# Attention stage: mask multiplies put ahead of the previous head's normalisation and of the scaling of V on VectorE

## The reference

```python
xn = layernorm(x)                                  # x: (4, 2048, 4096)
q = (xn @ Wq).reshape(B, S, 32, 128)
k, v = split(xn @ Wkv)                             # one key/value head of 128, shared by all 32 heads
scores = einsum('bqhd,bkd->bhqk', q, k) * 128**-0.5
scores = where(causal, scores + slope[h] * (kpos - qpos), -inf)
attn = einsum('bhqk,bkd->bqhd', softmax(scores), v)
W = (w_q - 128) * scales                           # one scale per 32 inputs, (4096, 4096)
out = x + attn.reshape(B, S, 4096) @ Wo + xn @ W.T
```

## Time and profile before

| what | value |
|---|---|
| time, median of two runs | 2699.53 us (2677.26 and 2721.8) |
| profiled execution, its own time | 2493.82 us |
| span of its slowest core (core 4) | 2492.3 us |
| spans of the eight cores | 2461.7 to 2492.3 us |
| granted TensorE clock, mean per core | 0.890 to 0.897 |
| busy, share of the span: TensorE matmuls, VectorE, ScalarE, GpSimd | 79%, 31%, 22%, 4% |
| first and last copy of row sums (line 684), stage C of core 4 | 777.5 and 1432.3 us |

### The profile page before, as it was taken

The page is one execution under the profiler, slowest core; times in us unless marked ns, Lnnn a source line. Parts: engine busy times, 40 slices in busy tenths (PEclk is TensorE's granted clock), DMA queues, the critical chain, the costliest instruction groups (busy, mean ns, idle before and its releaser), DMA issues.

```text
span 2492.3 us, 39192 instructions; the slowest of 8 cores (2461.7 to 2492.3 us)
## 1 busy us (share of the span) xinstructions
PE 1962.0 (79%) x15350; PEld 1429.2 (57%) x15451; DVE 776.1 (31%) x1896; ACT 538.9 (22%) x595; POOL 87.3 (4%) x103
## 2 busy tenths in 40 slices
PE   1555379999996666666666699899995699999999
PEld 1444234444443333333334388788884588888888
DVE  2666200000003555565444411111110544444432
ACT  0111000000003444445555500000000222222221
POOL 0000000000000000010000000000000000000000
PEclk9866689999997677758988899999997899999999
DMA  7432465676550000014000048867774866665522
GB/s 185 153 136 102 58 69 69 73 84 81 68 68 1 1 1 1 1 19 50 1 1 1 1 49 87 84 88 95 101 95 81 176 149 144 141 140 139 142 86 76
DMA packets 218274, 193.04 MB, mean 77 GB/s; under 512 B 9840, under 2 KB 210544, under 8 KB 211824
## 3 DMA queue, kind: packets, MB, share of 16 engines
q0 software_dynamic: 140736, 103.88, 32.8%
q1 hardware_dynamic: 77360, 86.66, 11.5%
HBM read 269.21 MB, written 25.17 MB: 118 GB/s over the span
## 4 chain that ended last, share of the span: by engine, by line
PE 67%; DVE 12%; DMA 8%; ACT 6%; issue 6%; DVEq 0%; ACTq 0%; POOL 0%; SPq 0%; POOLq 0%
PE psD L411 18%; PE psE L882 17%; PE psD L750 16%; PE psC_av L654 6%; ACT expb L551 5%; PE psC_sc L524 4%; DVE vf L506 3%; DMA wpan<-wo 3%; DVE lnst L261 2%; PE psE_tr L840 2%; PE psA_tr L299 2%; DMA wkvb<-wkv 2%; DMA wpan<-wq 2%; DVE xn_tm L280 1%; DMA scalesb<-scales 1%
## 5 line engine op out<-in xcount | busy, mean ns | idle before, releaser
L882 PE MATMUL psE<-wtp,xnt 128*128 128x256 bf16 x4096 | 469.7, 274 | 28.1 <-ACT wtp L850 22.6
L411 PE MATMUL psD<-xnt,wpan 128*128 128x512 bf16 x2007 | 441.7, 380 | 42.8 <-DMA wpan<-wq 40.6
L750 PE MATMUL psD<-wpan,qat 128*128 128x256 bf16 x4096 | 453.4, 275 | 15.2 <-DMA wpan<-wo 14.5
L750 PEld LDWEIGHTS psD<-wpan,qat 128*128 128x128 bf16 x4096 | 403.4, 99 | 65.1 <-issue 15.9
L882 PEld LDWEIGHTS psE<-wtp,xnt 128*128 128x128 bf16 x4096 | 396.6, 98 | 75.7 <-issue 30.6
L551 ACT ACTIVATE expb<-psC_sc 128x1024 bf16<-128x1024 f32 x333 | 327.1, 1013 | 331.9 <-PE psC_sc L524 304.7
L411 PEld LDWEIGHTS psD<-xnt,wpan 128*128 128x128 bf16 x2048 | 200.8, 98 | 283.8 <-issue 43.3
L654 PE MATMUL psC_av<-vf,expb 128*128 128x129 bf16 x1912 | 189.5, 251 | 190.0 <-DVE expb L562 90.3
L850 ACT COPY wtp<-psE_tr 128x1024 bf16<-128x1024 bf16 x128 | 129.0, 1012 | 900.2 <-PE psE_tr L840 900.2
L654 PEld LDWEIGHTS psC_av<-vf,expb 128*128 128x128 bf16 x1912 | 145.8, 113 | 284.0 <-issue 279.4
L524 PE MATMUL psC_sc<-qat,kt 128*128 128x512 bf16 x603 | 226.6, 474 | 6.0 <-issue 3.5
(11 more groups left out here) (49 smaller groups left out, 832.0 us busy)
## 6 DMA issues: line engine op xcount, KB each, us to landing
xblk<-x SPq DMA_DIRECT2D x16, 2048.0 KB, 7.8
wpan<-wq POOLq DMA_DIRECT2D x16, 2048.0 KB, 21.1
wpan<-wo POOLq DMA_DIRECT2D x16, 2048.0 KB, 24.2
wqr<-wqi POOLq DMA_DIRECT2D x32, 1024.0 KB, 10.3
xin<-x SPq DMA_DIRECT2D x128, 128.0 KB, 3.5
out<-outst SPq DMA_DIRECT2D x128, 128.0 KB, 2.1
scr_awo<-awo SPq DMA_DIRECT2D x128, 64.0 KB, 5.0
awin<-scr_awo SPq DMA_DIRECT2D x128, 64.0 KB, 2.8
```

The lines of the kernel that those rows point to most:

```text
L411: ins = e.matmul(psB[:, quarter * 512:(quarter + 1) * 512], wpan[:, bufp * 8192 + dt * 256 + sub * 128: bufp * 8192 + dt * 256 + (sub + 1) ...
L750: ins = e.matmul(psB[:, slot * 512: slot * 512 + 256], qat[:, h * 1024 + qb * 128: h * 1024 + (qb + 1) * 128], wpan[:, bufp * 8192 + h * 2 ...
L882: ins = e.matmul(psE[:, slot * 512: slot * 512 + 256], xnt[:, dt * 1024 + qb * 128: dt * 1024 + (qb + 1) * 128], wtp[:, bufp * 8192 + dt * ...
```

## The change

In each head the three VectorE steps behind evA are recorded in another order. Before: vf, evB, fm(0). After: fm(0), evB, vf. The waits of every step and all other engines' rows stay as they are. evB also stays in the same place relative to ctp.

```diff
--- before.py
+++ after.py
@@ -497,6 +497,7 @@
                 idx0 = r * NH + h
                 bufv = idx0 % 2
                 ve_vf = 0
+                vfb_todo = None
                 if h >= WIDE_H0:
                     def vfb(e, h=h, r=r, kbs=kbs, bufv=bufv):
                         ins = None
@@ -511,7 +512,7 @@
                     vfw = [("ldm", 32), ("ge", ge_ones)]
                     if idx0 >= 2:
                         vfw.append(("pe", last_av[idx0 - 2]))
-                    ve_vf = E.op("vector", vfb, wait=vfw, inc="ve")
+                    vfb_todo = (vfb, vfw)
                 for gi in range(G + 1):
                     if gi < G:
                         grp = groups[gi]
@@ -530,14 +531,6 @@
                         if it == 0:
                             waits += [("se", B_se)]
                         sc_pe = E.op("tensor", smm, wait=waits, inc="pe")
-                        if gi == 0 and pending is not None:
-                            i_p = pending["idx"]
-                            zr_p = E.reserve("ve")
-                            fn_p = pending["evB"]
-                            ve_evB[i_p] = E.op("vector",
-                                               lambda e, fn_p=fn_p, zr_p=zr_p: fn_p(e, zr=zr_p),
-                                               wait=[("ve", se_evA[i_p]),
-                                                     ("pe", pe_ctp.get(i_p - 2, 0))], inc="ve")
                         if gi == min(3, G - 1) and pending is not None:
                             i_p = pending["idx"]
                             pe_ctp[i_p] = E.op("tensor", pending["ctp"],
@@ -632,6 +625,18 @@
                                 fst["g"] = False
                             else:
                                 ge_f[it] = None
+                        if gi == 0:
+                            if pending is not None:
+                                i_p = pending["idx"]
+                                zr_p = E.reserve("ve")
+                                fn_p = pending["evB"]
+                                ve_evB[i_p] = E.op("vector",
+                                                   lambda e, fn_p=fn_p, zr_p=zr_p: fn_p(e, zr=zr_p),
+                                                   wait=[("ve", se_evA[i_p]),
+                                                         ("pe", pe_ctp.get(i_p - 2, 0))], inc="ve")
+                            if vfb_todo is not None:
+                                ve_vf = E.op("vector", vfb_todo[0], wait=vfb_todo[1], inc="ve")
+                                vfb_todo = None
 
                     if gi >= 1:
                         grp = groups[gi - 1]
```

## The result

The changed kernel takes 2554.82 us (median of 11 runs); the kernel before takes 2494.13 us (median of 10). The ratio is 1.0273, 95% interval 1.0239 to 1.0308: slower. The profiled execution took 2548.91 us.

What follows compares the result with a forecast made beforehand. VectorE's steps before AV(0), the first probability-times-V group, were taken to bound stage C's wide heads. The terms 22.8 + 27.1 + 2.4 + 8 = 60 us, added to 2699.5, gave 2759.5 us (+2.2%), range 2722 to 2795 us.

Steps and rivals of the forecast that it cites:

- The mechanism: Start of wide heads in stage C: vf used to cover exp(0), and now nothing does, so AV(0) comes later.
- Round 0, the later AV(0): 24 wide heads of round 0: AV(0) 0.95 us later each, 22.8 us, bounds 19 and 26.
- two phases of exp(0): Wide heads of round 0: exp(0) starts at T+0.61 or T+0.33 (T: evA's cast), making AV(0) 1.09 or 0.81 us late.
- Round 1: 24 wide heads of round 1: vf, and AV(0) waiting for it, 1.13 us later, 27.1 us, bounds 21 and 27.
- Narrow heads: 16 heads without vf: fm(1) 0.48 us late in five of them, 2.4 us; bounds a 5 us gain, 5 us more loss.
- The clock: TensorE at wide-head starts: longer idle makes more heads begin at 1.2 GHz, +8 us; bounds 20 loss, 30 gain.
- The rest of the program: Stages A, B, D and E: they keep every instruction and no other stage changes.
- The third rival: Every wide head starts at 1.2 GHz: +82 us, 2782 us; chance 0.13.
- The first rival: AV(0) to AV(1) of wide heads: the clock pays part of the delay back, +22 us, 2721.5 us; chance 0.11.
- the second: Round 1 absorbs the delay by slack later in the head: +33 us, 2732 us; chance 0.05.
- the fourth: Round 0: AV(0) follows fm(0) directly, vf being no wait, 1.17 us sooner, 28 us gained, 2671 us; chance 0.03.

## Why the prediction failed, and what held

The predicted 2759.5 us and its range of 2722 to 2795 miss the measured 2554.82. The step that failed is the last of the sum, the choice of the level to which the difference was added. I had both, the profiled execution's 2493.82 and the median of two runs, 2699.53, and carried the forecast, and the range with it, on the second. The runs showed 2494.13 as the median of ten; the same +60 us on the profile's level gave 2554. Two runs 44 us apart and 8% above a profiled execution of the same program should have counted as a warning about the two runs.

The mechanism held. VectorE idles 0.83 us in front of the first mask, vf starts at T+1.74 in round 1, AV(0) comes at T+4.70 in both rounds behind about 4.1 us of idle, and every other stage stays within 3 us. The mean wide head became 10.22 and 15.50 us, forecast 10.0 and 15.5.

The size was forecast a little low, at 1.022 to 1.024 where 1.0273 was measured. That 2554 lies within 1 us of 2554.82 is luck in part: the ratio makes 68 us, the mean span 63.7 and stage C 66.6, and not 60. The terms of the sum:

- Round 0, the later AV(0): 0.95 us a head forecast, 0.81 measured, 19 instead of 23 us. The lower of my two phases of exp(0), T+0.33, was by far the more frequent one (exp(0) starts at T+0.36 on average after the change), and I had taken the middle.
- Round 1: 1.13 forecast, 1.16 measured (T+4.70 as written). 28 us.
- Narrow heads: +2.4 us forecast, about 0 measured. Heads 3 to 5 of round 1 became 0.50 us longer (8.66 to 9.16) as reckoned, heads 6 and 7 stayed (11.06, 11.09), and heads 0 to 2 became shorter by 0.45 (6.49 to 6.04), which I had not counted; the share of slow AV(0) fell in them from 0.67 to 0.33.
- The clock: 8 us forecast, 20 measured (66.6 us of stage C less the 47 at equal clock). I put it in round 1 and "little" in round 0; it was the other way, 24 x 0.49 = 12 us in round 0 and 24 x 0.31 = 7 in round 1. In round 0 the share of slow AV(0) went from 0.57 to 0.97. The error was to read the granted 0.76 as "already low" and not to ask how many heads still began at the full clock.
- The rest of the program gave back 3 us, which I had put at nothing.

The first three came out 5 us lower together and the clock 12 higher, so the errors made up for each other only in part. The spread of 45 to 75 us left the narrow heads at 2.4; with the bounds that the prediction gives for them it would be 38 to 81.

The third rival (every wide head starts at 1.2 GHz) came true for nearly all heads of round 0 and for three fifths of round 1; its +82 us were not reached. The Trainium skill's rule on the gate ("TensorE: Matmul & The Clock Gate", section on HAM oscillation), that bursts parted by long idle gaps start at half clock each time, fits round 0 after the change (0.97 of the heads). It doesn't fit round 1, where two fifths of the heads start at 2.4 GHz behind an idle 4.1 us. The runs with extra matmuls show the other side: with twelve, which leave 1.5 us of idle in front of AV(0), the granted clock is 1.00.

The first rival (the clock pays back) and the second (round 1 absorbs the delay; at equal clock it passed on all of its 1.16 us) were wrong. So was the fourth (AV(0) follows fm(0) directly); it describes the order vf, fm(0), evB, which gained 28 us.

## What to carry to other kernels

In an in-order queue two steps that the same consumer needs are not equal if one is ready and the other waits: the ready one goes first, as cover, and what the consumer doesn't need (evB here) goes last. Better still, a ready step leaves the critical spot altogether; vf recorded one head earlier was worth 3.8%. And where some bursts of TensorE already start at the low clock, a longer gap is to be costed with the clock that it takes away, here 20 us on top of 47.

## What I had not expected of the hardware

Matmuls whose result nobody uses made a kernel faster: twelve per wide head, 576 in all, brought the changed kernel from 1.0273 to 1.0023 of the kernel before, with AV(0) no earlier. Part of that is a loss that the kernel before has too: six extra matmuls took its stage C from 652.8 to 620.3 us, by one profiled execution of each, about half of what the change cost. And idle gaps of one length, 4.08 us, ended at 1.2 GHz in one head and at 2.4 GHz in the next.
